# Layer 1 values computed transposed and turned back, key forms cleared after the outputs, last context stored by halves

## Reference

```
q  = jnp.dot(x, Wq).reshape(b, t, H, HD).transpose(0, 2, 1, 3)
kv = jnp.dot(x, Wkv).reshape(b, t, G, 2, HD).transpose(2, 3, 0, 1, 4)
k, v = (kv[:, 0], kv[:, 1])
...
scores = jnp.einsum('bhqd,bhkd->bhqk', q, k)
```

## Time and profile before

| | |
|---|---|
| median of 3 runs | 1756.12 us (1753.5 to 1759.4) |
| profiled execution, its own time | 1757.35 us |
| its span | 1755.6 us |
| mean granted TensorE clock | 0.979 |
| PE busy | 1650.3 us, 94% of the span |
| end of latent attention, last context copy | 1122.56 us from the span's start |
| first product of the outputs block | 1129.34 us |
| first product of grouped attention | 1286.14 us |

### The profile page before, as it was taken

One profiled execution on the slowest core, in us unless ns is written; L12 is line 12 of the kernel. 1 busy time (PEld: TensorE's weight loads), 2 busy tenths in 40 slices (PEclk: granted clock), 3 DMA queues, 4 the chain that ended last, 5 costly groups with the idle time before them and its releaser, 6 DMA issues. The chain is left out here.

```text
span 1755.6 us, 27326 instructions
## 1 busy us (share of the span) xinstructions
PE 1650.3 (94%) x8874; PEld 1232.9 (70%) x8874; DVE 1085.6 (62%) x2491; ACT 847.8 (48%) x1595; POOL 709.1 (40%) x735
## 2 busy tenths in 40 slices
PE   5899999999988999999999999799999999999998
PEld 5688887788777667766677766577765555568887
DVE  3545657999838677777777776345756777510222
ACT  3456556443326555555555555343135565653321
POOL 1112213444647566665566665385001111322221
PEclk9999999999999999999999999899969999999999
DMA  8522223221110001000001000463622342231111
GB/s 238 167 76 91 88 73 102 56 65 29 54 37 1 19 19 37 19 19 19 19 19 37 19 19 13 127 197 121 174 34 50 73 76 62 51 95 61 48 49 48
DMA packets 110716, 114.16 MB, mean 65 GB/s; under 512 B 39520, under 2 KB 71744, under 8 KB 110592
## 3 DMA queue, kind: packets, MB, share of 16 engines
q1 hardware_dynamic: 108288, 108.40, 22.2%
q10 hardware_dynamic: 2304, 4.20, 0.7%
HBM read 83.97 MB, written 28.44 MB: 64 GB/s over the span
## 5 line engine op out<-in xcount | busy, mean ns | idle before, releaser
L1447 ACT ACTIVATE a_p<-a_sm,a_nmax 128x640 f32<-128x640 f32 (+7 forms) x256 | 198.7, 778 | 142.9 <-DVE a_nmax L1408 141.3
L1490 POOL TENSOR_SCALAR a_p<-a_p,a_rinv 128x640 f32<-128x640 f32 (+7 forms) x256 | 190.6, 748 | 167.8 <-DVE a_rinv L1416 166.4
L1408 DVE CUSTOM_DVE_ANT_0 a_sm<-ps,maskb 128x640 f32<-128x640 f32 (+7 forms) x256 | 192.0, 750 | 100.4 <-PE ps L1352 98.4
L2334 DVE CUSTOM_DVE_ANT_0 ga_sm<-ps,strip 128x640 f32<-128x640 f32 (+1 forms) x224 | 163.3, 755 | 80.4 <-PE ps L2241 78.8
L2354 ACT ACTIVATE ga_pt<-ps 128x1024 f32<-128x1024 f32 (+1 forms) x192 | 148.1, 810 | 114.3 <-PE ps L2264 113.5
L1364 PE MATMUL ps<-ident,a_p 128*128 128x128 f32 x1152 | 172.5, 275 | 12.8 <-DVE a_pt L1423 12.5
L1364 PEld LDWEIGHTS ps<-ident,a_p 128*128 128x128 f32 x1152 | 132.8, 140 | 39.5 <-issue 16.9
L2394 POOL TENSOR_SCALAR_AFFINE_SELECT ga_pt<-ga_pt 128x512 f32<-128x512 f32 x64 | 40.6, 635 | 287.5 <-ACT ga_pt L2354 287.3
L1352 PE MATMUL ps<-kh,lq_qh 128*128 128x512 f32 (+3 forms) x384 | 129.0, 390 | 17.5 <-DVE a_nmax L1408 10.6
L923 DVE SCALAR_TENSOR_TENSOR idx<-ix_r,ix_sgc,idx 128x256 f32<-128x256 f32 (+6 forms) x105 | 90.8, 885 | 76.2 <-ACT ix_r L888 76.2
L1379 PE MATMUL ps<-a_pt,vst 128*64 128x512 f32 (+3 forms) x768 | 135.7, 496 | 1.8 <-DVE a_pt L1423 1.1
(11 more groups left out here) (319 smaller groups left out, 4015.2 us busy)
## 6 DMA issues: line engine op xcount, KB each, us to landing
ctx_d<-a_ctxst SPq DMA_DIRECT2D x16, 512.0 KB, 2.9
idx<-ctx_d SPq DMA_DIRECT2D x32, 256.0 KB, 3.7
idx<-wvo_d SPq DMA_DIRECT2D x32, 256.0 KB, 4.4
ga_qst<-qkd SPq DMA_DIRECT2D x42, 128.0 KB, 4.2
f_wr<-in_L_ffn_w SPq DMA_DIRECT2D x18, 256.0 KB, 2.7
x<-in_L_attn_hidden_states SPq DMA_DIRECT2D x16, 256.0 KB, 4.5
op_wo<-in_L_attn_o_w SPq DMA_DIRECT2D x8, 512.0 KB, 4.4
ix_w<-in_L_attn_idx_wq_w SPq DMA_DIRECT2D x64, 64.0 KB, 1.9
```

What stands on the lines that cost most here:

```text
L1408: dve.tensor_tensor_reduce(out=sm[kind][:, 0:w], in0=slots[kind][:, 0:w], in1=maskb[:, MASK_OFF[t]:MASK_OFF[t + 1]], scale=-scale, scalar= ...
L1447: act.activation(p[kind][:, v // 2 % 2, 0:w], sm[kind][:, 0:w], ACT.Exp, bias=nmax[:, v % 4:v % 4 + 1], scale=-1.0, accum_out=rsum[:, v % ...
L1490: pool.tensor_scalar(mine, mine, rinv[:, v % 4:v % 4 + 1], 1.0, ALU.mult, ALU.mult).then_inc(norm_done, 1)
L2334: dve.tensor_tensor_reduce(out=sm[kind][:, 0:w], in0=slots[kind][:, 0:w], in1=strip[:, S - w:], scale=-1.0, scalar=3.0e38, op0=ALU.add, op ...
```

## The change

Three edits.

1. The last task of each half is now `("T", 5, h)`, the values of 512 tokens at once, transposed: 12 products of 512 columns. ACT copies the result into a spare tile (`norm[2 + h]`, whose names in the trace are `sums`). Two V tasks at the end turn it back with four transposes of 128 columns each, and ACT copies 512 columns of values into `v32`. There are 14 tasks in place of 18. The narrow scores stand at tasks 8 and 9, the wide ones at tasks 10, 11 and 12.
2. POOL clears `kst` after all output steps with eight instructions: group 0 first, then groups 1 and 2. DVE clears nothing. One semaphore `formed` replaces `zero_a` and `zero_b`; SP waits for 4 of it before the first `load_group` of group 0 and for all 8 before that of group 1.
3. `ctxst` holds one half; the other half is in `kept`, a piece of `idx` that is unused then. SP stores each half by itself, with a semaphore each, and the block ends when the last *first* half has landed. In the outputs block SP waits for the half that it loads.

```diff
@@ latent_attention @@
-        ctxst = c.sb(tag + "_ctxst", [P, S])
+        ctxst = [c.sb(tag + "_ctxst", [P, HALF])[:, :], kept]
...
-                        act.wait_ge(ctx_out, START + i * 16)
-                    act.copy(ctxst[:, half * HALF:(half + 1) * HALF], ps[:, bank_c, :]).then_inc(ctx_done, 1)
+                        act.wait_ge(ctx_out[half], START + i * 16)
+                    act.copy(ctxst[half], ps[:, bank_c, :]).then_inc(ctx_done, 1)
...
-                    sp.wait_ge(ctx_done, START + 2 * i + 2)
-                    sp.dma_start(ctx_d[i], ctxst[:, :]).then_inc(ctx_out, 16)
-                sp.wait_ge(ctx_out, START + 16 * IT)
+                    for half in range(2):
+                        sp.wait_ge(ctx_done, START + 2 * i + half + 1)
+                        sp.dma_start(ctx_d[i][:, half * HALF:(half + 1) * HALF], ctxst[half]).then_inc(ctx_out[half], 16)
+                sp.wait_ge(ctx_out[0], START + 16 * IT)
@@ outputs_to_queries @@
-    tasks = [("T", m, 0) for m in (NQ, 0, 1, 2, 3)] + [("T", m, 1) for m in (NQ, 0, 1, 2, 3)]
-    tasks += [("V", t, 0) for t in range(ST)]
-    SMALL, BIG = (7, 8), (10, 11, 12, 13, 14)
-    LAST = 14
+    VALUES = NQ + 1
+    tasks = [("T", m, h) for h in range(2) for m in (NQ, 0, 1, 2, 3, VALUES)] + [("V", h, h) for h in range(2)]
+    SMALL = (8, 9)
+    BIG = [(10, 0), (10, 1), (10, 2), (10, 2), (10, 3), (11, 0), (11, 0), (11, 1), (11, 1), (11, 2), (11, 2), (11, 3), (11, 3),
+           (12, 1), (12, 2), (12, 3)]
+    LAST = 12
@@ SyncE @@
+                        sp.wait_ge(ctx_out[half], START + 16 * (k + 1))
                         load_outputs(sp, ctxn, ctx_d, wvo_d, raw_in, half, k)
...
-                            sp.wait_ge(zero_a, START + 2)
-                            sp.wait_ge(zero_b, START + 3)
+                            sp.wait_ge(formed, START + 4)
...
+                sp.wait_ge(formed, START + 8)
                 load_group(sp, qkd, qst, kst, q_in, k_in, 1)
@@ POOL, behind the loop over the output steps @@
+                for n, at in enumerate((slice(0, 1), slice(1, NB1))):
+                    for m, (rows, form, value) in enumerate(((slice(0, P), slice(0, 2), 0.0), (slice(KQ1, KQ1 + 1), 0, 1.0),
+                                                             (slice(KQ1, KQ1 + 2), 1, 1.0), (slice(KQ1, KQ1 + 1), 1, 0.0))):
+                        if n or m:
+                            pool.wait_ge(formed, START + 4 * n + m)
+                        pool.memset(f32(kst[rows, at, form]), value).then_inc(formed, 1)
@@ ACT @@
+                    if n in values:
+                        act.copy(norm[2 + h], ps[:, n % 4, :]).then_inc(hi_done, 1)
...
-                        act.copy(v32[:, m, :, 0:HD1], v).then_inc(hi_done, 1)
+                        act.copy(v32[:, 4 * h:4 * h + 4, :, 0:HD1], v).then_inc(hi_done, 1)
...
-                    if n == LAST + 1:
+                    if n == LAST:
@@ DVE, in the output steps @@
-                    if (half, k) == (0, 6):
-                        dve.memset(f32(kst[:, :, 0]), 0.0).then_inc(zero_a, 1)
-                    if (half, k) == (0, 8):
-                        dve.wait_ge(zero_a, START + 1)
-                        dve.memset(f32(kst[KQ1:KQ1 + 1, :, 0]), 1.0).then_inc(zero_a, 1)
@@ PE @@
+                    if kind == "V":
+                        pe.wait_ge(hi_done, START + values[h] + 1)
...
-                            ins = mm3(pe, ps[:, n % 4, 0:KD], (xnh[:, k, a1], xnl[:, k, a1]),
-                                      (wh[NQ + 1][:, k], wl[:, k, D + KD:]), k == 0, k == DT - 1)
+                            ins = pe.transpose(ps[:, n % 4, k * P:(k + 1) * P], norm[2 + h][:, k * P:(k + 1) * P], ident[:, :])
```

More of the change, by code:

```diff
@@ L110 @@
                            w2_in=2)
-ATTENTION0 = names("a0_", "scored max_done exp_done inv_done norm_done turned ctx_done weighed ctx_out", pt_done=3)
+ATTENTION0 = names("a0_", "scored max_done exp_done inv_done norm_done turned ctx_done weighed", pt_done=3, ctx_out=2)
 ATTENTION0 += names("lq_", "raw_in tab_in wh_done wl_done q_mm q_evac add_done qh_done q_lo_done")
@@ L114 @@
 TO_QUERIES = names("oq_", "x_done stat var_done std_done rstd_done xn_done turned xh_done xl_done wh_done wl_done done "
[L115 removed]
+                   "hi_done lo_done ones_done formed", split_done_=4, cl_done_=4, wvl_done_=4, used_=4, stored=5,
                    w_in=2)
@@ L1270, in lora_ffn, with latent_attention @@
         c.finish()
-def latent_attention(nc, tag, ps, maskb, scale, kh, kl, vst, qwork, ctx_d, load_first, renew):
+def latent_attention(nc, tag, ps, maskb, scale, kh, kl, vst, qwork, ctx_d, kept, load_first, renew):
     IT = H // 2
@@ L1293, in latent_attention @@
         pt_done = c.sems(tag + "_pt_done", NT)
-        weighed, ctx_out = c.sem(tag + "_weighed"), c.sem(tag + "_ctx_out")
+        weighed, ctx_out = c.sem(tag + "_weighed"), c.sems(tag + "_ctx_out", 2)
         slots = [ps[:, 0:2, :].rearrange("p b n -> p (b n)"), ps[:, 2, :]]
@@ L1737, in outputs_to_queries @@
 def outputs_to_queries(nc, c, ps, ident, x, ctx_d, wvo_d, raw_in, xnh, xnl, wq, wkv, qkd, v32, ctxn, raw, sums, qst, kst, q_in,
-                       k_in, strip, nmax, nT, first, ahead):
+                       k_in, strip, nmax, nT, first, ahead, ctx_out):
     NS = OUT_SLOTS
@@ L1760, in outputs_to_queries @@
     for v in range(UNITS1 // 2):
-        n, k = divmod(v * 5 // 4, DT)
-        places.setdefault((BIG[n], k), []).append(UNITS1 // 2 + v)
+        places.setdefault(BIG[v], []).append(UNITS1 // 2 + v)
     TURNED = 4
-    lows = [n for n, task in enumerate(tasks) if task[0] == "T"]
+    values = [n for n, task in enumerate(tasks) if task[:2] == ("T", VALUES)]
+    lows = [n for n, task in enumerate(tasks) if task[0] == "T" and n not in values]
     with ExitStack() as st:
@@ L1785, in outputs_to_queries @@
         names = ("x_done", "stat", "var_done", "std_done", "rstd_done", "xn_done", "turned", "xh_done", "xl_done",
-                 "wh_done", "wl_done", "done", "hi_done", "lo_done", "ones_done", "zero_a", "zero_b")
+                 "wh_done", "wl_done", "done", "hi_done", "lo_done", "ones_done", "formed")
         (x_done, stat, var_done, std_done, rstd_done, xn_done, turned, xh_done, xl_done, wh_done, wl_done, done,
-         hi_done, lo_done, ones_done, zero_a, zero_b) = (c.sem("oq_" + n) for n in names)
+         hi_done, lo_done, ones_done, formed) = (c.sem("oq_" + n) for n in names)
         split_done, cl_done, wvl_done, used = (
@@ L2038, in task @@
                                       k == 0, k == DT - 1)
-                            if k == DT - 1:
-                                ins.then_inc(done, 1)
-                        else:
-                            a1 = slice(m * P, (m + 1) * P)
-                            ins = mm3(pe, ps[:, n % 4, 0:KD], (xnh[:, k, a1], xnl[:, k, a1]),
-                                      (wh[NQ + 1][:, k], wl[:, k, D + KD:]), k == 0, k == DT - 1)
-                            if k == DT - 1:
-                                ins.then_inc(done, 1)
+                        else:
+                            ins = pe.transpose(ps[:, n % 4, k * P:(k + 1) * P], norm[2 + h][:, k * P:(k + 1) * P], ident[:, :])
+                        if k == DT - 1:
+                            ins.then_inc(done, 1)
                         for v in places.get((n, k), ()):
@@ L2734, in two_layers @@
                                    v32, ctxn, rest["raw"], rest["sums"], qst, kst, q_in, k_in, strip, nmax, nT, first,
-                                   ahead)
+                                   ahead, [Ctx.named[f"a0_ctx_out{h}"] for h in range(2)])
                 grouped_attention(nc, ps, ident, strip, qkd, raw_d, inv_d, v32, ctxn, qst, kst, q_in, k_in, rest, nmax,
```

15 lines of the change are left out of this document (4 added, 11 removed).

## The result

The changed kernel took 1744.9 us (median of 6 runs, 1742.27 to 1747.91), the kernel before beside it 1757.76 (6 runs, 1753.5 to 1765.28): ratio 0.9933, interval 0.9911 to 0.9954. Two further comparisons gave 0.9923 [0.9903, 0.9943] and 0.9970 [0.9951, 0.9989]. It is faster, by 0.3 to 0.8%. The intervals of the last two do not overlap; they were measured on two chips, and why the gain differs is open. Three runs stand far apart from all others of their kernels (5450.34 us in `a2_after`, 2289.18 in `e11_scores_held`, 1852.15 in the kernel before beside `e8_clear_values`) and are left out of every median here.

The account below looks back on a forecast made before the run. PE, busy 94% of the span, was taken to bound the kernel, so its work, waits and clock count. Gains of 2.3 + 5.4 + 0.6 = 8.3 us gave a forecast of 1748, range 1743 to 1754.

Parts of the forecast that it names:

- the likeliest case: Whole kernel: measurably faster, chance 0.67, against 0.28 for the same and 0.05 for slower.
- Seam: Between last context copy and next block: stores by halves remove the wait for the last store's landing, 2.3 us.
- Rival A: At the seam: the block's end itself waits for transfers under way, so the 2.3 us stay; 1750, chance 0.1.
- Clearing: Output step 8: without clearings ahead of POOL's remainder, PE's 4.15 us stall and 1.3 of slow products go, 5.4 together.
- rival B: Output steps 12 to 15: PE stops for a load, half of the 5.4 us comes back; 1750.5, chance 0.1.
- Cost 0; the cover is POOL's idle time: Behind the output steps: the eight moved clearings, 13.7 us with their waits, cost nothing.
- Rival C: Last clearings beside DVE's norm of tiles 4 and 5: they collide, PE loses up to 2.7 us; 1750.5, chance 0.08.
- Values: Tail before grouped attention: 8.1 us behind the last maximum become 4.0, maxima end 3.5 later, gain 0.6 us.
- Rival D: First wide score: the landing wait drops the clock, which returns late, up to 7 us; 1752 to 1755, chance 0.12.
- E: Slower: the whole wide-score stretch at half clock and the next block's low clock lasting on; about 1762, chance 0.05.
- The low clock behind: Start of grouped attention, 1286 to 1306: low clock stays; each us shorter or longer counts up to 0.5.
- signs of being wrong: PE waiting at steps 8 to 15; clock 0.5 during wide maxima; grouped attention after 1281; later low clock not 20 us.

Follow-up runs that it names:

- a2_after: The changed kernel once more, unchanged, run for comparison on the same chip as two-edit kernels: 1748.19 us.
- e11_scores_held: The changed kernel with the first half's value product later, the second clearings held until normalization ends, and scores started earlier: 1747.46 us, ratio 0.9964.
- e8_clear_values: The kernel before with the clearing and values edits, without the stores by halves: 1746.79 us, ratio 0.9939.
- e10_clear_held: The kernel before with the clearing edit alone, its second half held until DVE has written the last normalized row: 1753.34 us, ratio 0.9972.
- e4_stores_clear: The kernel before with the stores by halves and the clearing edit, without the values edit: 1759.94 us, ratio 1.0031.
- a1_after: The changed kernel once more, unchanged, run beside the kernels with one edit each: 1746.86 us, ratio 0.9923.
- e7_fill: The changed kernel with extra 512-column products that nobody reads, behind the last wide scores and the last transposes: 1748.79 us, ratio 0.9960.
- e2_clear: The kernel before with the clearing edit alone, POOL's eight clearings behind the output steps: 1760.10 us, ratio 1.0009.

## Why the prediction was right, point by point

- **Forecast 1748 (1743 to 1754), measured 1744.9**, and 1746.86 and 1748.19 in the later comparisons. The kernel got faster, as the likeliest case had it.
- **Seam, 2.3 us**: 2.2 in every kernel with the stores by halves. Rival A falls.
- **Clearing, 5.4 us**: the output steps shorten by 4.9, by 5.6 in `e10_clear_held`. At the start of the steps the clock is low for 4.3 us in the kernel after and for 2.9 and 3.0 in the kernel before and `e10_clear_held`, which takes the 0.7 back; how much of that low stretch falls on the steps is chance, 3.0 to 5.6 us over the kernels without the stall. No load became the next wait, so rival B falls. "Cost 0; the cover is POOL's idle time" was the error: POOL was free, DVE was not. Rival C came true, with its price read wrongly. DVE's delay did not reach PE through the norm, where PE has slack; it went through the remainder and SP's queue to the landing. The Trainium skill, "SBUF — State Buffer" (SBUF: two separate sides), says of a POOL instruction and a DVE instruction in a two-port mode that the one that starts first blocks the other for its whole length. The rows agree: the addition starts 0.38 us into a clearing of 1.80 us and ends 0.04 us behind it. Whether it runs in such a mode no row says.
- **Values, 0.6 us: the term that was mis-sized.** In the profiles the tail came out 0.45 us longer in the kernel after and 1.0 shorter in `a2_after`, so as a difference from the kernel before the 0.6 is as good as a measurement here can tell. Its mechanism was read rightly: a wait of 1.55 us (up to 2.4 was forecast), 4.63 us from the last maximum to grouped attention (4.0), its start at 1278.19 (near 1278, of which the 1.2 us ahead of the seam are chance). Added to the kernel before, the edit gives 1.0 us in the median, within the interval. But it was priced against the tail of the kernel before, at full clock. With the clearing in place the alternative is `e4_stores_clear`: 11.8 us slower than the kernel after on the same chip, by a tail of 68.2 us. Its worth is the clock that it saves.
- **Rival D** happened in small: the clock falls behind the wait in the kernel after and in `a1_after` (tails 59.30 and 59.37) and not in `a2_after`, `e8_clear_values` and `e7_fill` (57.82, 57.35 and 57.65), so it costs 1.5 to 2 us. What spoke against it, that the wide scores and 512-column products bring it back, held with both together; the wide scores with V products of 128 columns between them did not do it in `e2_clear`. The transposes did not bring the clock down among the last wide scores: it was 1.00 until 1273. D in full, and E's sign, is what `e4_stores_clear` shows.
- **The low clock behind** was forecast to stay 20 us long and lasted 15.8. The rest of the program is 2.2 us shorter for it, and that is chance: `a1_after`, the same program, has 33 us, and the other kernels without filling lie between 14 and 26.
- **The sum of 8.3** lies under the first two differences of medians (12.9 and 10.3) and near the third (7.7); by the ratios the three are 11.8, 13.5 and 5.3. That it holds so well is luck in part. The clearing was priced at no cost outside the output steps, and its real cost, a tail 9.3 us longer, was kept away only by the values edit, which was taken in for 0.6. And 1.2 us ahead of the seam and 2.2 behind the tail came by chance.
- **Of the signs of being wrong** two were there: a low clock of 3.4 us while the wide maxima ran, and a low stretch behind them of another length than 20 us. Both are too small to change the forecast.

## What to carry to other kernels

A short wait of PE is priced by what PE does behind it: a wait of 1.9 us and the low clock behind it cost 9 where products of 128 columns and scores followed; where 512-column products did, the clock fell for 3.4 us or not at all, and that cost nothing to 2 us beyond the wait. Work moved onto an idle engine can have a price on the engine that it disturbs (here 1.3 us on one addition); follow that engine's next results to the queue that waits for them. Where edits of one change lie within one stretch of time, measure them in pairs as well as alone: here -2.9, +3.0 and -1.0 made -10.3.

## What the runs showed of the hardware that was not expected

- In two kernels (`e2_clear`, `e4_stores_clear`), one profiled execution each, the granted clock stayed at 0.50 for 44 us though PE was busy for 28.54 of 30 us in the first, with no idle time in its rows from 1254 to 1275. Its work in these 44 us began with 86 products of 128 columns and 26 products of wide scores, of 128 to 512 columns. With 512-column products in place of those of 128 the clock was back after 3.4 us. In `e10_clear_held` the same products of 128 columns, reached at 2.4 GHz, kept 1.00 from 1250 to 1272: in these traces they hold the clock but did not restore it. Whether it is their width, their order or the places of the scores was not separated. The Trainium skill, "TensorE: Matmul & The Clock Gate" (Part 4), says that transposes don't count as busy in the same way; these were products, so that does not explain it.
- A clearing on POOL stretches DVE's addition over 4 columns from 0.17 to 1.46 us and two normalized rows from 1.00 to 2.09.
- Code that differs in the stores at most reaches the same instruction at moments up to 9.5 us apart, for the most part by how long the clock was low until then (17.1 us in the earliest, 41.0 in the latest).
